# First attention of a two-layer kernel: three PSUM banks for short-lived products and three tiles of scores

## The reference, cut to what matters

```python
x = L0_attn_x                                   # (8, 1024, 128)
h = _layernorm(x, axis=-1) * (1 + ca) + sa
x = x + ga * _L0_attn_ref(h, Wq, Wk, Wv)
...
def _L0_attn_ref(x, Wq, Wk, Wv):                # H, R = 8, 64
    Q = (x @ Wq.T).reshape(b, n, H, R)
    K = (x @ Wk.T).reshape(b, n, H, R)
    V = (x @ Wv.T).reshape(b, n, H, d)
    attn = jnp.einsum('bnhr,bmhr->bhnm', Q, K)
    attn = jax.nn.softmax(attn, axis=-1)
    out = jnp.einsum('bhnm,bmhd->bnd', attn, V)
    return out
```

## Time and profile before

| | us |
|---|---|
| median of 3 runs | 3081.31 |
| range of the runs | 3079.63 to 3084.49 |
| the profiled execution | 3079.73 |
| its span, first to last instruction | 3077.9 |

### The profile page before, as it was taken

One profiled execution on the slowest core, in us unless ns is written; L12 is line 12 of the kernel. 1 busy time (PEld: TensorE's weight loads), 2 busy tenths in 40 slices (PEclk: granted clock), 3 DMA queues, 4 the chain that ended last, 5 costly groups with the idle time before them and its releaser, 6 DMA issues. The chain is left out here.

```text
span 3077.9 us, 77592 instructions
## 1 busy us (share of the span) xinstructions
PE 2810.5 (91%) x27940; PEld 2083.9 (68%) x27940; DVE 2286.6 (74%) x8471; ACT 2189.3 (71%) x4273; POOL 1779.8 (58%) x1756
## 2 busy tenths in 40 slices
PE   5999999999999999999999995699998999898688
PEld 3777777777777777777777775466666666666443
DVE  6676776776766767767767645899999999997565
ACT  3888788788888887887887780565666666666575
POOL 3778777778778778778778781333333333332121
PEclk7999999999999999999999997687787787777799
DMA  3000000000000000000000001100000000000000
GB/s 102 1 1 8 1 1 8 1 1 8 1 1 8 1 1 8 1 1 8 1 1 8 1 1 63 66 0 0 0 0 0 0 0 0 0 0 2 8 21 28
DMA packets 11793, 27.63 MB, mean 9 GB/s; under 512 B 1529, under 2 KB 6137, under 8 KB 11137
## 3 DMA queue, kind: packets, MB, share of 16 engines
q1 hardware_dynamic: 11618, 25.48, 2.4%
HBM read 17.07 MB, written 8.40 MB: 8 GB/s over the span
## 5 line engine op out<-in xcount | busy, mean ns | idle before, releaser
L284 POOL TENSOR_TENSOR probs_l<-probs,probs_h 128x512 fp32r<-128x512 f32 x1024 | 1302.7, 1291 | 378.6 <-ACT probs_h L378 377.4
L377 ACT ACTIVATE probs<-bank 128x512 f32<-128x512 f32 x1024 | 625.8, 611 | 323.3 <-PE bank L698 297.0
L539 DVE TENSOR_REDUCE maxes<-ring 128x1 f32<-128x512 f32 x1024 | 659.0, 686 | 177.0 <-PE ring L678 176.2
L378 ACT ACTIVATE probs_h<-bank 128x512 fp32r<-128x512 f32 x1024 | 625.2, 611 | 0.0
L697 PE MATMUL bank<-q_hh,k_hl 128*128 128x512 f32 x1024 | 423.8, 414 | 0.2 <-ACT q_lm L367 0.2
L698 PE MATMUL bank<-q_lm,k_h 65*128 65x512 f32 x1024 | 405.1, 396 | 0.0
L708 PE MATMUL obank<-probs_h,x_l 128*128 128x512 f32 x1024 | 403.9, 394 | 0.0
L710 PE MATMUL obank<-probs_h,x_h 128*128 128x512 f32 x1024 | 402.8, 393 | 0.0
L709 PE MATMUL obank<-probs_l,x_h 128*128 128x512 f32 x1024 | 402.4, 393 | 0.0
L678 PE MATMUL ring<-k_hl,q_hh 128*128 128x512 f32 x1024 | 378.8, 430 | 24.5 <-DVE k_hl L523 6.0
L1074 ACT ACTIVATE low_hot<-obank 128x512 f16<-128x512 f32 x512 | 297.0, 604 | 66.7 <-PE obank L1249 53.6
(11 more groups left out here) (252 smaller groups left out, 4971.0 us busy)
## 6 DMA issues: line engine op xcount, KB each, us to landing
xt<-in_x SPq DMA_DIRECT2D x8, 512.0 KB, 10.2
out_x<-xt SPq DMA_DIRECT2D x8, 512.0 KB, 2.6
x<-out_x SPq DMA_DIRECT2D x1, 4096.0 KB, 12.2
out_x<-x SPq DMA_DIRECT2D x16, 256.0 KB, 2.1
mod<-out_x SPq DMA_DIRECT2D x3, 512.0 KB, 13.7
pk_wq<-in_w_q SPq DMA_DIRECT2D x1, 1024.0 KB, 4.8
pk_wqT<-in_w_qT SPq DMA_DIRECT2D x1, 1024.0 KB, 6.9
hot_rule<-in_hot_rule SPq DMA_DIRECT2D x1, 776.0 KB
```

Source lines behind the costliest of these rows:

```text
L284: nc.gpsimd.tensor_tensor(probs_l[:, i, :], probs[:, s % 4, :], probs_h[:, i, :].bitcast(F32), ALU.subtract).then_inc(low_ready, 1)
L377: nc.scalar.activation(probs[:, s % 4, :], st[s % 4], ACT.Exp)
L378: nc.scalar.activation(probs_h[:, i, :], st[s % 4], ACT.Exp).then_inc(st_free[s % 4], 1)
L539: nc.vector.tensor_reduce(maxes[:, i, k:k + 1], ring[bank_of(at)][:], AX.X, ALU.max).then_inc(rows_maxed, 1)
```

## The change

The second half of `bank2[1]`, the fourth score tile, becomes a third bank of the ring. Uses of the ring go to bank `at % 3`, and TensorE waits for the release of the use three places back. The score tiles become three, taken in turn over the whole run of steps (`score_use` gives tile and number of use from n = 16 g + s), so that TensorE waits before scores for the exponentials of three steps back. The other engines' waits are counted anew for the same events.

```diff
-        st = [bank2[i // 2][:, (i % 2) * HALF:(i % 2 + 1) * HALF] for i in range(4)]
+        st = [bank2[i // 2][:, (i % 2) * HALF:(i % 2 + 1) * HALF] for i in range(3)]
+        ring = [*ring, bank2[1][:, HALF:N]]
...
-        ring_full = [sem(f"ring_full{r}") for r in range(2)]
+        ring_full = [sem(f"ring_full{r}") for r in range(3)]
...
-        st_full = [sem(f"st_full{r}") for r in range(4)]
-        st_free = [sem(f"st_free{r}") for r in range(4)]
+        st_full = [sem(f"st_full{r}") for r in range(3)]
+        st_free = [sem(f"st_free{r}") for r in range(3)]
...
         def bank_of(at):
-            return at % 2
+            return at % 3
 
         def filled(at):
-            return at // 2 + 1
+            return at // 3 + 1
...
+        def score_use(g, s):
+
+            n = 2 * TB * g + s
+            return n % 3, n // 3
...
                 if g >= 2:
-                    pool.wait_ge(st_full[3], 4 * (g - 1))
+                    last, use = score_use(g - 2, 2 * TB - 1)
+                    pool.wait_ge(st_full[last], use + 1)
...
             def low_part(g, s):
                 i = s % DEEP
-                pool.wait_ge(st_free[s % 4], 4 * g + s // 4 + 2)
+                bank, use = score_use(g, s)
+                pool.wait_ge(st_free[bank], use + 2)
...
-                act.wait_ge(st_full[s % 4], 4 * g + s // 4 + 1)
-                nc.scalar.activation(probs[:, s % 4, :], st[s % 4], ACT.Exp)
-                nc.scalar.activation(probs_h[:, i, :], st[s % 4], ACT.Exp).then_inc(st_free[s % 4], 1)
+                bank, use = score_use(g, s)
+                act.wait_ge(st_full[bank], use + 1)
+                nc.scalar.activation(probs[:, s % 4, :], st[bank], ACT.Exp)
+                nc.scalar.activation(probs_h[:, i, :], st[bank], ACT.Exp).then_inc(st_free[bank], 1)
...
-                if at >= 2:
-                    sem_, count = released(at - 2)
+                if at >= 3:
+                    sem_, count = released(at - 3)
                     pe.wait_ge(sem_, count + 1)
                 return ring[bank_of(at)]
...
-                if g or s >= 4:
-                    pe.wait_ge(st_free[s % 4], 4 * g + s // 4 + 1)
+                bank, use = score_use(g, s)
+                if use:
+                    pe.wait_ge(st_free[bank], use + 1)
...
-                nc.tensor.matmul(st[s % 4], k_hl[w][:, keys], q_hh[w][:, queries], start=True, stop=False)
-                nc.tensor.matmul(st[s % 4], k_h1[w][:, keys], q_lm[w][:, queries], start=False, stop=True).then_inc(st_full[s % 4], 1)
+                nc.tensor.matmul(st[bank], k_hl[w][:, keys], q_hh[w][:, queries], start=True, stop=False)
+                nc.tensor.matmul(st[bank], k_h1[w][:, keys], q_lm[w][:, queries], start=False, stop=True).then_inc(st_full[bank], 1)
```

## The result

| | before | changed |
|---|---|---|
| median of 7 runs, us | 3083.78 | 3066.77 |
| range | 3074.36 to 3089.40 | 3061.29 to 3078.38 |
| profiled execution | 3079.73 | 3061.36 |
| span | 3077.9 | 3059.6 |
| first to last score start (the attention) | 55.0 to 1846.6 | 54.5 to 1820.3 |

The ratio is 0.9953 (95% interval 0.9937 to 0.9969): 0.5% faster, and the interval keeps clear of no change. The forecast was 3058 and faster; the measured time lies in the range, 9 us above the forecast. The gain itself was forecast at 23.1 us; it is 17.0 by the two medians and 14.5 (10 to 19) by the ratio. In the profile the attention lost 25.8 us, and 8 came back in code that the change does not touch.

A forecast was written before the change was run, and what follows sets the result against it. TensorE was taken to bound the kernel, stalled in plain heads by takes of the two-bank ring. Terms of -33.0 + 8.7 + 1.2 = -23.1 us gave 3056.6 for the profiled execution, 3058 for the median; range 3044 to 3074.

The forecast's parts named there:

- The ring: Third ring bank lets s = 5 of a plain head start at 8.24, not 8.84: 0.60 us in 55 heads, 33.0 us.
- The tiles: With three score tiles, s = 3 waits for the exponentials of s = 0, 0.46 us later; 0.43 falls into the ring's saving.
- Without that cover: If the ring's saving did not absorb the wait at s = 3, it would cost 62 x 0.46 = 29 us.
- h = 6 and 7: End of h = 6 gives nothing, as s = 3 of h = 7 waits for exponentials; h = 7 still gives 0.60 us.
- h = 0: Seven heads with b over 0: turn_max waits for row_max behind GpSimd's subtractions, 1.24 us lost each, 8.7 us.
- row_max gets in only where GpSimd has nothing waiting: At h = 0 row_max waits until GpSimd's subtraction ends at 755.38, so L686 starts at 755.46, not 754.22.
- the outcome that had a chance of 0.04: Rival: row_max gets in at the first change of subtraction, the 1.12 stall gone too; -45 us, 3036, chance 0.04.
- the term for a held-up head: Each h = 0 head with b over 0 loses 1.24 us as L686 starts later, and its 0.60 gain.
- The 1.2 us booked for the first head: First head of all: row_max pushed by the same rule, from 0 to 1.2 us possible, 1.2 taken.
- h = 2: In h = 2 heads L720 of s = 2 no longer waits 1.6 us for k_hl; 0.60 us a head counted.
- The rest carried over unchanged: Code after the attention's score steps, not touched by the change: its 1230 us stay the same.

The follow-up runs named there:

- two pairs of kernels: Two ring banks and four tiles against three and three: with row_max as a reduction 3073.75 against 3043.14; with the norm also moved 3061.29 against 3026.73.
- two tiles: Four ring banks and two score tiles in place of three and three, on the changed kernel with row_max as a reduction; 3225.32, ratio 1.0451.
- one run: Changed kernel with elementwise row_max, GpSimd leaving out the low parts of the value tiles for all batches but the first; 3049.08, ratio 0.9846.
- its form with the reduction: Changed kernel with row_max taken by one tensor_reduce over both halves instead of an elementwise maximum of two SBUF inputs; 3043.14, ratio 0.9864.
- four profiles: Kernel before (3083.78), changed kernel (3066.77), and changed kernel with a memset ahead of row_max, tiny (3062.51) or 128x512 (3057.13).
- a fifth: Changed kernel with GpSimd leaving out the low parts of the value tiles after the first batch; 3049.08, ratio 0.9846.

## Why the prediction was right, and where it was off

- **The ring (33.0 us from 55 heads).** Right in mechanism and size: 0.60 a plain head, 30.6 and 34.6 us for the whole change of banks and tiles by two pairs of kernels that differ in nothing else, 33.0 for the third ring bank alone.
- **The tiles (absorbed at s = 3).** Right: s = 3 at 4.75, s = 5 unmoved with two ring banks. "Without that cover" showed with two tiles, where the wait is 2.3 us a head: plain heads are 1.9 us longer, and those with half clock 3.5.
- **h = 6 and 7.** Right as a pair, 8.7 for 9.0.
- **h = 0.** The mechanism was right (two SBUF inputs against a GpSimd queue that is behind; row_max 5.0 us, TensorE 2.95): taking away the second SBUF input ends it in every head. That the queue is what holds row_max is less sure, since in one run it got in seven times of seven with the queue still there. The step that failed is "row_max gets in only where GpSimd has nothing waiting". In the profile four of seven got in at the first change, the outcome that had a chance of 0.04, and gave 1.85 us each instead of losing 1.24. And the term for a held-up head was too small: it lasts 31.6 us, 2.8 over 28.8, not 1.24, since 1.54 of half clock comes on top. The two errors have opposite signs. The 1.2 us booked for the first head came as 0.8, by luck: row_max wasn't held up there, and 6.8 us at half clock cost it instead (with the reduction for row_max and 3.4 us of it, that head lasts 25.0). In the profile the h = 0 heads cost 1.8 us together, against 9.9 forecast. In the median run they cost more: the changed kernel stands 0.9% above its form with the reduction, some 27 us, which at 4.67 each would be about six held-up heads rather than three (an estimate; only the profiled run shows its heads). Six would also account for some 6 of the 9 us by which the gain by the ratio, 14.5, stays behind the 23.1 forecast.
- **h = 2.** 4.8 us were booked and 1.2 came. Half clock behind TensorE's pause takes 1.24 us in three heads of the changed kernel; the sum had no term for the clock, since the kernel before shows no half clock in the attention. Moving the norm took away both the pause and the half clock.
- **The rest carried over unchanged.** It took 1239.3 us for 1231.3 in the two profiles. The profiles of the ten experiments show 1232 to 1239 for the same code, so this is the spread of that part, and the profile of before lay at its lower end. The attention and its start, 26.3 us sooner, would have given 3053.4 for the profiled execution; these 8 us make it 3061.4. Their cause was not tried.

## What to carry to other kernels

Before a buffer is moved from one ring to another, draw the few microseconds in which both are late on one time axis: here the wait that was taken on and the wait that was given up lay in the same gap, and the sum was right to 0.05 us a head. A 128x8 operation with two SBUF inputs can last through four operations of the other engine (5.02 us here); as a reduction, with one input, it takes 0.17 us. And when a change shifts TensorE against a contended engine, count what one long pause costs afterwards at half clock, not the pause alone.

## What the runs showed of the hardware

- A VectorE instruction with two SBUF inputs was held up by more than one GpSimd instruction: 3.19 us over three subtractions, 5.02 over four; the 4.88 us of wv_gated look the same. The Trainium skill (SBUF — State Buffer, "SBUF: two separate sides") has a block for the whole instruction, and with instructions back to back that bounds the wait too low. Whether the waiting one gets in at a change varied: 8 of 8, 3 of 7, 4 of 7 and 6 of 8 were held up in four profiles, the first heads counted in the first and the last, and 0 of 7 in a fifth, with a backlog that at the change was about that of the first.
- TensorE's clock fell from 2.4 to 1.2 GHz, for 3.4 or 6.8 us at a time, in or behind the pauses of 2.26, 2.95 and 4.09 us shown above, and in some h = 2 heads behind one of 1.24; in the kernel before, pauses of 1.6 and 1.12 us passed without. The length of the pause alone doesn't decide.
